# Layer 1's projections on the array's halves, with more of the splitting on DVE

## The reference

```python
zn = _sparse_norm(z, alpha_in, beta_in)
a = jax.nn.sigmoid(_lin(zn, W_ga, b_ga)) * _lin(zn, W_la, b_la)
b = jax.nn.sigmoid(_lin(zn, W_gb, b_gb)) * _lin(zn, W_lb, b_lb)
k = jnp.einsum('bitc,bjtc->bijc', a, b)
kn = _sparse_norm(k, alpha_o, beta_o)
return jax.nn.sigmoid(_lin(zn, W_go, b_go)) * _lin(kn, W_lo, b_lo)
```

## Time and profile before

| | |
|---|---|
| time, median of 3 runs | 1039.27 us (1038.81 to 1039.66) |
| the profiled execution's own time | 1042.83 us |
| its span, first to last instruction | 1040.9 us |
| busy, PE / DVE / ACT / POOL | 89% / 73% / 65% / 46% |
| projections of layer 1, chunk 1: first product to first matrix product | 725.32 to 765.42 us |
| matrix products of chunk 1 | 765.42 to about 787.3 us |

### The profile page before, as it was taken

The page is one execution under the profiler, slowest core; times in us unless marked ns, Lnnn a source line. Parts: engine busy times, 40 slices in busy tenths (PEclk is TensorE's granted clock), DMA queues, the critical chain, the costliest instruction groups (busy, mean ns, idle before and its releaser), DMA issues.

```text
span 1040.9 us, 40845 instructions
## 1 busy us (share of the span) xinstructions
PE 927.0 (89%) x16740; PEld 743.7 (71%) x16740; DVE 763.9 (73%) x1276; ACT 673.4 (65%) x1104; POOL 476.6 (46%) x416
## 2 busy tenths in 40 slices
PE   5857877799999999978999996899999999869997
PEld 5732334698888988867898995678878788635554
DVE  5765898776868768688999998755646556458886
ACT  4659883566656666565777774575857758447775
POOL 0002667780752916506877882580936719200000
PEclk9879997799999999999999997899999999889999
DMA  9900000003113021179998940006032050389995
GB/s 333 377 23 2 2 2 2 3 4 121 45 43 122 4 106 60 49 215 261 223 217 192 219 91 1 3 4 163 4 89 78 7 160 4 89 200 294 359 325 192
DMA packets 159905, 122.06 MB, mean 117 GB/s; under 512 B 70788, under 2 KB 136708, under 8 KB 157704
## 3 DMA queue, kind: packets, MB, share of 16 engines
q1 hardware_dynamic: 159752, 119.74, 40.2%
HBM read 69.38 MB, written 50.33 MB: 115 GB/s over the span
## 4 chain that ended last, share of the span: by engine, by line
PE 74%; DVE 8%; ACT 6%; DMA 4%; issue 3%; POOL 2%; SPq 1%; DVEq 0%; POOLq 0%; ACTq 0%
PE PS L524 64%; PE PS L826 3%; DMA AB<-x 3%; PE PS L841 3%; ACT XT_ALL L931 2%; PE PS L873 2%; ACT AB L936 2%; PE PS L538 1%; POOL AB L377 1%; DVE AB L1359 1%; DMA AB<-k_scratch 1%; DVE XT_ALL L1361 1%; DVE XT_ALL L1529 1%; ACT WK L971 1%; SPq L391 1%
## 5 line engine op out<-in xcount | busy, mean ns | idle before, releaser
L524 PE MATMUL PS<-EFF,XT_ALL 64*128 64x64 f16 (+1 forms) x11112 | 326.3, 199 | 8.3 <-POOL XT_ALL L1105 3.2
L524 PEld LDWEIGHTS PS<-EFF,XT_ALL 64*128 64x128 f16 (+1 forms) x11112 | 296.6, 97 | 50.7 <-issue 25.8
L524 PE MATMUL PS<-AB 64*128 64x128 bf16 (+2 forms) x2058 | 239.9, 287 | 28.2 <-DVE XT_ALL L1361 13.0
L524 PEld LDWEIGHTS PS<-AB 64*128 64x128 bf16 (+2 forms) x2058 | 200.2, 123 | 68.5 <-issue 22.1
L971 ACT ACTIVATE WK<-PS,T 128x512 f32<-128x512 f32 x256 | 174.4, 685 | 94.8 <-PE PS L524 83.4
L1169 POOL TENSOR_TENSOR AB<-WK,AB 128x512 f32 x128 | 145.1, 1165 | 111.0 <-ACT AB L981 110.2
L377 POOL TENSOR_TENSOR AB<-WK,MS 128x512 f32 x96 | 130.6, 1390 | 105.5 <-DVE WK L1397 105.4
L1105 POOL TENSOR_TENSOR XT_ALL<-AB,XT_ALL 128x512 f16<-128x512 f32 x60 | 71.1, 1188 | 125.4 <-DVE XT_ALL L1361 120.4
L1405 DVE TENSOR_TENSOR WK<-PS,WK 128x512 f32<-128x512 f32 x128 | 85.8, 687 | 31.8 <-ACT WK L971 31.6
L1397 DVE TENSOR_TENSOR WK<-PS,WK 128x512 f32<-128x512 f32 x128 | 86.7, 689 | 30.2 <-ACT WK L971 25.0
L1421 DVE BATCH_NORM_STATS2 REC<-WK 128x512 f32 x64 | 44.5, 695 | 59.6 <-ACT WK L1000 59.6
(11 more groups left out here) (199 smaller groups left out, 1435.5 us busy)
## 6 DMA issues: line engine op xcount, KB each, us to landing
AB<-x SPq DMA_DIRECT2D x64, 512.0 KB, 6.9
p_scratch<-WK SPq DMA_DIRECT2D x32, 512.0 KB, 2.6
k_scratch<-WK SPq DMA_DIRECT2D x128, 128.0 KB, 1.9
AB<-k_scratch SPq DMA_DIRECT2D x32, 512.0 KB, 11.1
out<-AB SPq DMA_DIRECT2D x16, 1024.0 KB, 7.6
AB<-p_scratch SPq DMA_DIRECT2D x29, 512.0 KB, 8.0
AB<-p_scratch SPq DMA_DIRECT2D x2, 640.0 KB, 5.7
AB<-spread SPq DMA_DIRECT2D x1, 896.0 KB, 7.4
```

Source lines behind the costliest of these rows:

```text
L524: return nc.tensor.matmul(dst, lhsT, rhs, start=start, stop=stop)
```

## The change

Four things are changed, all in layer 1:

1. All eight of eight units are split (`SPLIT_ROWS[1]`).
2. `HIGHS_V` is (1, 3): DVE makes the high parts of units 1, 3, 5 and 7 of eight, ACT those of 0, 2, 4 and 6.
3. DVE also makes the low part of unit 6 of eight (`LOW_V`), after its product of unit 7. POOL makes the other seven. A new semaphore `ablo_done_v` counts DVE's.
4. The waits for high and low parts count accordingly (`highs`, `lows_before`).

```diff
-SPLIT_ROWS = ((0, 2, 4, 6), (0, 2, 3, 5, 7))
+SPLIT_ROWS = ((0, 2, 4, 6), tuple(range(8)))
...
-        HIGHS_V = (3,)
+        HIGHS_V = (1, 3)
         HIGHS_A = 4 - len(HIGHS_V)
+
+        def highs(u):
+
+            return sum((w % 4 in HIGHS_V) == (u % 4 in HIGHS_V) for w in range(u + 1))
+
+        LOW_V = 6
+
+        def lows_before(n8, u):
+
+            if u == LOW_V:
+                return ablo_done_v, n8 + 1
+            return ablo_done, n8 * (UB - 1) + u + (u < LOW_V)
...
-                        pe.wait_ge(ablo_done, (q + 1) * NP)
+                        pe.wait_ge(ablo_done, (q + 1) * (NP // UB * (UB - 1)))
+                        pe.wait_ge(ablo_done_v, (q + 1) * (NP // UB))
...
-                            reached(act, ablo_done, n - (UB - 1))
+                            reached(act, *lows_before(q * (NP // UB) + n8 - 1, u))
...
                     for u in range(UB):
-                        made = u // 4 + 1 if u % 4 in HIGHS_V else u // 4 * HIGHS_A + u % 4 + 1
+                        if u == LOW_V:
+                            continue
+                        made = highs(u)
                         fours = q * (NP // 4) + n8 * (UB // 4)
                         if u % 4 in HIGHS_V:
-                            pool.wait_ge(abhi_done_v, fours + made)
+                            pool.wait_ge(abhi_done_v, fours * len(HIGHS_V) + made)
...
                             V.tensor_tensor(gate, lin, gate, ALU.mult).then_inc(prod_done[1], 1)
+                            if u == LOW_V + 1:
+                                dve.wait_ge(abhi_done, (q * (NP // 4) + n8 * (UB // 4)) * HIGHS_A + highs(LOW_V))
+                                V.tensor_tensor(ab_rows(ab_lo, n8, LOW_V), sig1[:, LOW_V], ab_rows(ab_hi, n8, LOW_V),
+                                                ALU.subtract).then_inc(ablo_done_v, 1)
```

More of the change, by code:

```diff
@@ L289, in build @@
         ablo_done = sem("ablo_done")
+        ablo_done_v = sem("ablo_done_v")
         p_in = [sem(f"p_in{s}") for s in range(2)]
```

## The result

Measured: **1050.39 us** (median of 4 runs, 1049.74 to 1052.92) against 1039.47 us for the kernel before on the same chip (1038.81 to 1039.78, 4 runs). The ratio is 1.0114 with a 95% interval of 1.0102 to 1.0126: 10.9 us slower, where 10.8 us faster had been forecast. The profiled execution took 1050.84 us.

A forecast was written before the change was run, and what follows sets the result against it. PE was taken to set the pace, POOL close behind; after the change DVE, at 9.03 us for eight units. 2.7 us per chunk, 10.8 for four, off the profiled span, brought to the median: 1028.5 us, range 1020 to 1036.

The forecast's parts named there:

- PE: ... Eight units now take 7.44 us: Layer 1's projections: three whole units of eight go from 1.75 to 0.93 us on PE, 2.45 us less.
- PE with 7.44 of 9.03 has more [to spare]. The pace is DVE's.: Layer 1's projections: DVE sets 9.03 us for eight units; POOL has 0.6 us to spare, PE more.
- PE 0.93 per split unit: Layer 1's projections: a split unit takes PE 0.93 us, a whole one 1.75.
- The chain of DVE and ACT, 1.97 for two units: Layer 1's projections: product to high part 0.73, to sigmoid 0.54, to next product 0.70 us; two units can't take less.
- The low part's wait for POOL: Unit 6's low part on DVE waits for POOL's current instruction: 0.52 us in the first eight units, 0.36 later.
- The cost to POOL's next low part: After DVE's low part, POOL's next low part waits 0.59 us, a figure taken from layer 0's masks.
- The gain of 2.7 us per chunk: Each chunk, first product to first matrix product: 37.41 us instead of 40.10; 10.8 us gained over four chunks.
- the matrix products don't stay at 21.9 us: The matrix products after each chunk's projections: the prediction had them unchanged at 21.9 us.
- The first rival, the relief nearly whole: Layer 1's projections: DVE and ACT run closer than the chain says, POOL is the bound; 1018 to 1022 us, chance 0.14.
- Evacuation takes it back: Engines behind PE fall out of step, eight units need 9.6 to 9.9 us as before; 1034 to 1044, chance 0.17.
- The clock falls: PE's short idles in layer 1's projections lower its clock; half the stretch at half clock gives 1059 us; chance 0.07.
- What would show it: Signs in layer 1's projections; wrong if DVE's low part takes 0.68, a PE unit near 1.8, or POOL never idles.

The follow-up runs named there:

- two_in_48: two_products with each second product cut into two matmuls of 32 columns, so a unit again has 48 small matmuls: 1055.46 us, ratio 1.0163 to the kernel before.
- two_products: The changed kernel without the third product (low part of x times high part of the weights) in layer 1's projections: 1029.55 us, ratio 0.9912 to the kernel before.
- before_800: The kernel before with its whole units' 128-column matmuls cut into two of 64, 800 instructions for eight units instead of 656: 1055.36 us, ratio 1.0164.
- dve_only: The changed kernel with five of eight units split, as before, keeping the work moved to DVE: 1037.95 us, ratio 0.9994 to the kernel before.
- the four slow kernels: The kernels with 800 PE instructions in eight units, the changed kernel among them: medians 1050.4, 1055.5, 1053.8 and 1055.4 us.
- two_in_40: two_products with only every other row's second product cut into two matmuls of 32 columns, 84 instructions per unit: 1030.15 us, ratio 0.9904 to the kernel before.
- six_even: The changed kernel with units 3 and 7 of eight whole and six split, 704 instructions for eight units: 1043.87 us, ratio 1.004 to the kernel before.

## Why the prediction was wrong

The step that failed is "PE: ... Eight units now take 7.44 us", and with it "PE with 7.44 of 9.03 has more [to spare]. The pace is DVE's." The durations in it were right (a unit 0.92), but their sum is a pace only while PE's instructions are there. With 800 of them in eight units the supply sets the pace, near 11 us (the changed kernel's units that start at 744.93 and 755.85 are eight apart, 10.92 us). two_in_48 against two_products shows it with the columns held, before_800 with the other engines' work and the split units as before, and dve_only rules out the part of the change on the other engines.

The prediction should have seen it. It counted columns and microseconds on PE and never instructions, although the count was in the windows that it read (1312 matmuls and 1304 loads in 41.4 us, 63 instructions per us), and the step to 100 instructions in 0.93 us is 108 per us, beyond anything that the trace of before holds for long (at most 74 per us over any 256 instructions). The queue of instructions stood on the page (131 transfers), and blocks started 3.4 to 4.5 us apart in chunk 1's projections: busier than the queue's share of 0.9% suggests, which is taken over sixteen DMA engines and the whole span. None of the rivals was about supply, so the whole range lay on the wrong side.

Point by point:

- **PE 0.93 per split unit:** right when fed (0.92 after, at a granted clock of 1.00).
- **The chain of DVE and ACT, 1.97 for two units:** right. 0.73 and 0.54 as before; eight units in two_products come every 8.87 us, where 8.95 and 9.03 were forecast.
- **The low part's wait for POOL:** right in kind, a little large: 0.39 and 0.19 us over 0.68 (0.52 and 0.36 forecast). In the changed kernel most low parts take 0.68, since a starved POOL is idle when they come:

```profile
L1424 DVE TENSOR_TENSOR AB<-WK,AB x16: 680/680/1068, 664.8 to 900.1; 128x512 f32 x16
```

- **The cost to POOL's next low part:** 1.40 us for one of 1.16 where the two meet (766.51 above): 0.24, well under the 0.59 taken from layer 0. "SBUF — State Buffer" of the Trainium skill, section "Who interferes with whom", gave the direction, and the rows agree with it: only an overlap lengthens either of them, and never by a whole instruction here.
- **The gain of 2.7 us per chunk:** what it would be without the limit shows in two_products: 34.9 us from first to last low part, 35.6 forecast (37.41 less the 1.56 ahead of it and the 0.26 behind it), 38.3 before. Its median is 1029.6, beside the forecast 1028.5; that kernel isn't the one forecast, but it has the same work behind PE. That the two times lie so close is partly luck. The four stretches are 2.6 us shorter together than forecast, but the matrix products don't stay at 21.9 us as the prediction had it: PE waits 3.15 us for POOL before the first three, and they take 23.52 us, with the clock at its half level for 3.4 us of each.
- **The first rival, the relief nearly whole:** out also where PE is fed. **Evacuation takes it back:** its range holds none of the four slow kernels, and where PE stalls it waits neither for DVE nor for POOL. **The clock falls:** out for the changed kernel. PE stands for 28% of chunk 1's stretch, up to 1.3 us at a time (1.6 in the other chunks) and every 3.6 us, and the granted clock is 1.00 in the stretches of all four chunks. "TensorE: Matmul & The Clock Gate" of the Trainium skill, section "A second HAM failure mode: psum-queue depth-cycling", let one expect an oscillating clock from such gaps; no chunk's stretch of the changed kernel shows it, but two_in_48, with nearly the same stalls, does (0.81 and 0.96, above). What makes the difference isn't shown.
- **What would show it:** the signs named for a wrong forecast were a fast low part, a slow unit and a POOL without idle time. The sign that came, PE idle for "issue" inside a unit, was not among them.

The interval of the blocks follows the length of the transfers: in chunk 0 of the changed kernel nine in a row take 1.33 to 1.43 us and start 3.7 to 4.1 us apart, in chunk 1 they take 0.93 to 1.38 and start 3.45 to 3.8 apart. This makes chunk 0 the longest of the four, by 3 to 5 us. Open stays why the transfers take longer there, and what the engine does in the 1.2 to 1.4 us between the end of a transfer and PE's next matmul.

## What to carry to other kernels

Count PE's instructions per us beside its columns: a matmul and its weight load are two, and cutting a matmul in half, by array tiling too, doubles them. Here 63 to 66 per us were free, 74 could be had for some 25 us after a stretch of large matmuls (814 matmuls and 816 loads in 22 us of two_in_40), and more than that came out as stalls; where a change crosses the limit, take only as much of it as the supply bears (six of eight units split gain 0.3% in two of three orders, eight lose 1.1%). An idle PE with "issue" as its releaser in the middle of a group, at even intervals of instructions, is the sign.

## What the runs showed of the hardware

- PE's instructions come by DMA in blocks of 16 KB, 256 instructions (2304 more instructions, 9 more transfers; 768 more, 3 more). A block takes mostly 0.9 to 1.4 us to come, and under full demand one starts every 3.45 to 4.0 us in most cases: 64 to 74 instructions per us. In chunk 1 of the changed kernel the next transfer starts 1.05 to 1.17 us after PE has begun the block before, so more is not brought in ahead.
- The stalls are mostly 0.7 to 1.6 us each, 256 instructions apart, 42 of them and 46.9 us in the changed kernel.
- Some instructions lie ready after a stretch with few: after the matrix products PE ran 716 instructions, 2.8 blocks, in 8.1 us before its first stall (seven units and eight matmuls from 724.36 to 732.5). One block of these landed meanwhile, at 728.28.
- PE idle for 28% of a stretch, in gaps of up to 1.3 us, kept a granted clock of 1.00 in the changed kernel; in two_in_48, idle for 32% between 728 and 766 us, it was 0.96.
- The matrix products of a chunk take 21.92 us at a granted clock of 1.00. In six_even and two_products those of the first three chunks take 23.52 at 0.93, after PE has waited 2.0 to 2.1 and 3.15 us for POOL; in two_in_40 one takes 24.67 after 1.60, another 21.92 after 1.75.
